# Row marks by 64 small operations that carry the pick's code, in the list part of a hybrid attention and mixture-of-experts kernel

## The chip, the cores and the metric

The kernel runs on one core of one Trainium2 chip. The time is device microseconds of one execution; three runs of the kernel before took 1725.3, 1726.1 and 1726.22 us, so its median is 1726.1 us. The trace is of one further execution, which took 1725.6 us, and whose span from the first to the last instruction is 1723.9 us.

## The reference

The input is x of 4 x 1024 rows with 256 columns, float32. Four layers follow each other, each added to x: a causal attention with 16 heads of 16 (`a`), a mixture of experts (`ffn`), an attention of 8 x 512 rows with one head of 256 (`b`), and the same mixture of experts again. Each is fed a layer norm of x. What matters here is the mixture of experts, which stands twice:

```python
def _moe(t, gate_w, gate_b, mlp1_w, mlp1_b, mlp2_w, mlp2_b):
    logits = t @ gate_w + gate_b                 # 4096 rows, E = 8 experts
    top_v, top_i = jax.lax.top_k(logits, K)      # K = 2 picks for each row
    probs = jax.nn.softmax(top_v, axis=-1)
    w = jnp.zeros((T, E), t.dtype).at[jnp.arange(T)[:, None], top_i].set(probs)
    def body(acc, ew):
        w1, b1, w2, b2, we = ew
        h = _swiglu(t @ w1 + b1)
        y = h @ w2 + b2
        return (acc + we[:, None] * y, None)
```

## The kernel before, in words

The kernel is written engine by engine: each phase is a block in which every engine has its own program, in the order in which the code issues it, and semaphores connect them. No scheduler stands between. At the end of a block all engines meet. The phases are the projections (`a1_`), attention a (`a2_`), its output rows and the logits (`a3_`), the list part (`r1_`), the experts (`e1_`), attention b with its logits (`b_`), the list part again (`r2_`) and the experts again (`e2_`). The trace leaves out the digits: `r_` is the list part in both places, `e_` the experts.

Each of the 4096 rows has two picks, so there are 8192 picks, which lie as 128 partitions by Q = 64 columns. The experts don't compute all rows for all experts: the picks are sorted by expert into MT = 71 tiles of 128 slots, and a tile is computed with one expert's weights. The list part (`rank`, L1132) works out for each pick the slot that it goes to, and then turns this round: for each slot, which pick is in it. The result is the list `token` (128 x 71), which the gathers of the experts need.

Turning it round is a sum of 64 matrix products into one accumulator `p_inv` (128 rows of a tile by 71 tiles). Column q of the picks gives a 128 x 128 matrix of row marks (for each pick a 1 in the column of its row within the tile: `in_row`) and a 128 x 71 matrix of tile marks (a 1 in the column of its tile). Before the change the tile marks are multiplied by the pick's code (`g["marks"]`, a 16 bit integer read as bfloat16), and the product puts the code at its slot (L1340).

The marks are made in five groups of 8, 16, 16, 16 and 8 picks (`BOUNDS`), through two buffers each. The work of a group is shared:

- ScalarE (ACT) spreads the row numbers, each repeated 128 times, into `spread` (L1198).
- VectorE (DVE) compares `slot_tile` with a ramp of tiles into `in_tile` (L1269), multiplies that by the codes into `marked` (L1283), and compares `spread` with the ramp 0 to 127 into `in_row` (L1275). All are `tensor_tensor` operations over 568 to 2048 bfloat16 elements of each partition.
- TensorE (PE) waits for a group's `marked` and `in_row`, and issues its 8 or 16 products.

Behind the marks VectorE adds four tiles of the residual (`X<-X,R`, L1300, `held_added`), and then makes `token` from `p_inv` (L1305), which waits for the last product and for `rows_landed`. GpSimd (POOL) then gathers the first rows (L1367), TensorE turns them (L1459), ScalarE copies them (L1513), and the products of the experts begin (L1470). Beside this ScalarE waits for `held_added` and copies the first expert's weights (L1206).

Of the kernel before, what the change touches and what calls it, by code (L numbers as in the profile page):

```python
# [9 lines left out]
ALU = mybir.AluOpType  # L10
# [1121 lines left out]
def rank(nc, mem, g, t_dram, w_dram, normals):  # L1132
# [3 lines left out]
    QQ = 16  # L1136
    BOUNDS = (0, 8, 24, 40, 56, 64)
# [12 lines left out]
    slot_row = mem.sb("slot_row", [P, Q], BF16)  # L1150
    ramp_tile = mem.sb("ramp_tile", [P, MT, QQ], BF16)
    spread = mem.sb("spread", [P, 2, QQ, P], BF16)
    in_row = mem.sb("in_row", [P, 2, QQ, P], BF16)
    in_tile = mem.sb("in_tile", [P, 2, MT, QQ], BF16)
    marked = mem.sb("marked", [P, 2, MT, QQ], BF16)
# [12 lines left out]
    b_in, ramp_done, slots_done, spread_done, row_done, tile_done, mark_done, inv_done, token_done = (  # L1168
        mem.sem(s) for s in ("b_in", "ramp_d", "slots_d", "spread_d", "row_d", "tile_d", "mark_d", "inv_d", "token_d"))
# [3 lines left out]
    with nc.Block(no_gpsimd_drain=True) as block:  # L1173
# [14 lines left out]
        def _(act):  # L1188
            act.wait_ge(diff_done, 1)
# [3 lines left out]
            act.wait_ge(slots_done, 1)  # L1193
            for k in range(GROUPS):
                n = BOUNDS[k + 1] - BOUNDS[k]
                if k >= 2:
                    act.wait_ge(row_done, k - 1)
                act.copy(spread[:, k % 2, 0:n], slot_row[:, BOUNDS[k]:BOUNDS[k + 1]].unsqueeze(2).to_broadcast([P, n, P])  # L1198
                         ).then_inc(spread_done, 1)
# [9 lines left out]
        def _(dve):  # L1209
# [52 lines left out]
            def at(k):  # L1262
                return slice(BOUNDS[k], BOUNDS[k + 1]), k % 2, BOUNDS[k + 1] - BOUNDS[k]

            def tiles_of(k):
                picks_at, s, n = at(k)
                if k >= 2:
                    dve.wait_ge(mark_done, k - 1)
                dve.tensor_tensor(in_tile[:, s, :, 0:n], slot_tile[:, picks_at].unsqueeze(1).to_broadcast([P, MT, n]),  # L1269
                                  ramp_tile[:, :, 0:n], ALU.is_equal).then_inc(tile_done, 1)  # L1270

            def rows_of(k):
                picks_at, s, n = at(k)
                dve.wait_ge(spread_done, k + 1)
                dve.tensor_tensor(in_row[:, s, 0:n], spread[:, s, 0:n], g["ramp"][:, :].unsqueeze(1).to_broadcast([P, n, P]),  # L1275
                                  ALU.is_equal).then_inc(row_done, 1)

            def marks_of(k):
                picks_at, s, n = at(k)
                if k >= 2:  # L1280
                    dve.wait_ge(inv_done, k - 1)
                dve.wait_ge(tile_done, k + 1)
                dve.tensor_tensor(marked[:, s, :, 0:n], in_tile[:, s, :, 0:n],  # L1283
                                  g["marks"][:, picks_at].unsqueeze(1).to_broadcast([P, MT, n]), ALU.mult
                                  ).then_inc(mark_done, 1)

            tiles_of(0)
            for k in range(GROUPS):
                marks_of(k)
                if k == 0:  # L1290
                    tiles_of(1)
                rows_of(k)
                if k + 2 < GROUPS:
                    tiles_of(k + 2)
# [8 lines left out]
            dve.wait_ge(inv_done, GROUPS)  # L1303
# [12 lines left out]
        def _(pe):  # L1316
# [18 lines left out]
            for k in range(GROUPS):  # L1335
                pe.wait_ge(mark_done, k + 1)
                pe.wait_ge(row_done, k + 1)
                for q in range(BOUNDS[k], BOUNDS[k + 1]):
                    i = q - BOUNDS[k]
                    mm = pe.matmul(p_inv[:, 0:MT], in_row[:, k % 2, i, :], marked[:, k % 2, :, i],  # L1340
                                   start=(q == 0), stop=(q == Q - 1))
# [1077 lines left out]
```

## Time and profile before

| what | value |
|---|---|
| median of three runs | 1726.1 us |
| time of the profiled execution | 1725.6 us |
| its span | 1723.9 us |
| TensorE busy | 1619.6 us (94%), 11174 instructions |
| VectorE busy | 1271.0 us (74%), 2670 instructions |
| ScalarE busy | 1048.6 us (61%) |
| GpSimd busy | 790.2 us (46%) |
| first list part | starts at 647.4 us, its `token` at 669.30 us |
| second list part | starts at 1294.2 us, its `token` at 1316.13 us |

A busy TensorE is not one at its peak, since products are pipelined. Busy shares are means over the whole span; the two list parts are 22 us each of 1724. A row of the timeline gives the start in us, how long the piece is in us, the engine, the line, the operation, its output and inputs, the partitions by elements and their type, and how many instructions are merged in it. The pieces of one engine overlap: the next instruction starts before the one ahead of it has left the pipeline. So there are two readings of an instruction's cost, its duration and the time from its start to the start of the next.

### The profile page before, as it was taken

What the parts mean: (1) busy time and instruction counts of PE and PEld (TensorE: products, weight loads), DVE (VectorE), ACT (ScalarE), POOL (GpSimd) and SP (SyncE); (2) the same over time, 40 slices, a digit from 0 to 9 for tenths busy, and PEclk for the clock granted to TensorE, in tenths of its full rate; (3) what the DMA queues carried; (4) which work ended last, traced back from release to release, by engine and by line L of the source; (5) the groups of instructions that cost most, each with busy time, mean ns of one, the idle gap of its engine ahead of it and who ended that gap; (6) DMA issues with size and microseconds to landing.
All of it is one profiled execution on the core that took longest, in us unless ns stands there. A gap on an engine that the chain in (4) does not pass through costs nothing. (4 is left out here: it accounts for less than half of the span.)

```text
span 1723.9 us, 35933 instructions
## 1 busy us (share of the span) xinstructions
PE 1619.6 (94%) x11174; PEld 1195.5 (69%) x11175; DVE 1271.0 (74%) x2670; ACT 1048.6 (61%) x1850; POOL 790.2 (46%) x768
## 2 busy tenths in 40 slices
PE   8889999999999896999999997799976999999998
PEld 4454444444443685999999997445455999999997
DVE  5688888888884596777777775368897777777775
ACT  4436776776778465666666664557665666666663
POOL 4541111111121132666666664225632766666674
PEclk9999999999999896999999999899976999999999
DMA  5655354453531672332223332301122332222332
GB/s 163 184 148 125 101 129 114 112 125 99 137 105 45 160 248 59 72 49 46 46 48 49 49 47 36 110 1 52 49 74 67 49 49 46 47 47 49 49 48 35
DMA packets 102683, 140.85 MB, mean 82 GB/s; under 512 B 18176, under 2 KB 86784, under 8 KB 99520
## 3 DMA queue, kind: packets, MB, share of 16 engines
q1 hardware_dynamic: 65282, 90.53, 20.0%
q0 software_dynamic: 31808, 37.32, 13.6%
q10 hardware_dynamic: 5502, 11.88, 2.0%
q8 instruction: 45, 0.74, 0.2%
q14 instruction: 46, 0.38, 0.1%
HBM read 74.21 MB, written 56.69 MB: 76 GB/s over the span
## 5 line engine op out<-in xcount | busy, mean ns | idle before, releaser
L633 DVE TENSOR_REDUCE mx<-a_p_sn 128x2 f32<-128x256 f32 (+1 forms) x600 | 333.5, 627 | 60.9 <-PE a_p_sn L670 51.4
L607 ACT ACTIVATE a_Pt<-a_p_st 128x512 f32<-128x512 f32 (+2 forms) x606 | 294.0, 592 | 123.9 <-PE a_p_st L689 123.6
L1521 ACT COPY R<-values_then_w 128x1024 f32 x280 | 279.0, 1044 | 28.2 <-issue 22.2
L1470 PE MATMUL e_p_g<-e_tT,R 128*128 128x128 f32 x2272 | 280.0, 277 | 0.9 <-ACT e_tT L1513 0.9
L1470 PE MATMUL e_p_l<-e_tT,R 128*128 128x128 f32 x2272 | 277.0, 275 | 0.0
L1482 PE MATMUL e_p_y<-w,e_hid 128*128 x1136 | 270.1, 381 | 5.8 <-DVE e_hid L1588 5.8
L1470 PEld LDWEIGHTS e_p_g<-e_tT,R 128*128 128x128 f32 x2272 | 267.8, 194 | 1.8 <-ACT e_tT L1513 1.7
L1470 PEld LDWEIGHTS e_p_l<-e_tT,R 128*128 128x128 f32 x2272 | 265.5, 192 | 0.1
L584 POOL TENSOR_SCALAR_AFFINE_SELECT a_Pt<-a_Pt 128x512 f32<-128x512 f32 x128 | 81.5, 637 | 356.7 <-ACT a_Pt L607 356.7
L1482 PEld LDWEIGHTS e_p_y<-w,e_hid 128*128 128x128 f32 x1136 | 205.6, 191 | 28.4 <-issue 6.2
L670 PE MATMUL a_p_sn<-Kst,Qst 96*128 96x128 bf16 (+1 forms) x720 | 220.0, 332 | 1.8 <-PEq L161 1.8
L689 PE MATMUL a_p_st<-Qst,Kst 99*128 99x512 bf16 (+2 forms) x744 | 205.3, 329 | 6.8 <-DMA Qst<-a_mT 4.1
L1367 POOL DMA_INDIRECT xs<-t_rows,token x142 | 156.6, 1103 | 87.3 <-DVE token L1305 42.0
L1542 ACT ACTIVATE e_sig<-e_glu 128x512 f32<-128x512 f32 x142 | 89.5, 630 | 154.3 <-DVE e_glu L1574 84.5
L1572 DVE TENSOR_TENSOR e_glu<-e_p_g,b 128x512 f32<-128x512 f32 x142 | 98.2, 691 | 106.8 <-PE e_p_g L1470 93.1
L1373 POOL DMA_INDIRECT wt<-pick_weights,pick x142 | 147.7, 1040 | 43.3 <-issue 43.3
L1439 POOL DMA_INDIRECT out<-e_y,result x71 | 115.7, 1629 | 93.0 <-ACT e_y L1529 89.9
L1439 POOL DMA_INDIRECT x_rows<-e_y,result x71 | 115.7, 1630 | 92.0 <-ACT e_y L1529 84.9
L1578 DVE TENSOR_TENSOR e_lin<-e_p_l,b 128x512 f32<-128x512 f32 x142 | 98.2, 692 | 77.0 <-PE e_p_l L1470 75.0
L1529 ACT ACTIVATE e_y<-e_yb,wt 128x256 f32<-128x256 f32 x142 | 72.1, 508 | 129.4 <-DVE e_yb L1555 125.7
L704 PE MATMUL a_p_o<-a_Pt,a_Vst 128*32 128x512 f32 (+3 forms) x1536 | 137.4, 490 | 0.7 <-POOL a_Pt L584 0.7
L670 PEld LDWEIGHTS a_p_sn<-Kst,Qst 96*128 96x128 bf16 x720 | 70.0, 98 | 83.1 <-DVE mx L633 33.8
(266 smaller groups left out, 2381.0 us busy)
## 6 DMA issues: line engine op xcount, KB each, us to landing
qk_parts<-a_part SPq DMA_DIRECT2D x64, 192.0 KB, 3.2
a_Vst<-values_then_w SPq DMA_DIRECT2D x16, 512.0 KB, 18.4
values_then_w<-in_mlp SPq DMA_DIRECT2D x16, 512.0 KB, 4.4
t_rows<-R SPq DMA_DIRECT2D x16, 512.0 KB, 3.2
Kst<-qk_parts SPq DMA_DIRECT2D x14, 384.0 KB
Qst<-qk_parts SPq DMA_DIRECT2D x14, 384.0 KB
o_rows<-a_OT ACTq DMA_DIRECT2D x16, 256.0 KB, 2.0
o_rows<-xs ACTq DMA_DIRECT2D x16, 256.0 KB, 8.0
```

The lines of the kernel that those rows point to most:

```text
L607: act.activation(weights(kb, slice(h, h + n), a, b), key_scores(u, i)[:, 0:n * (b - a)].rearrange("p (n w) -> p n w", n=n), ACT.Exp, scale ...
L633: dve.tensor_reduce(mx[:, hs[0]:hs[-1] + 1, place], p_sn[:, (s + k) % RING, 0:w * len(hs)].rearrange("p (h w) -> p h w", w=w), AX.X, ALU.m ...
L670: mm = pe.matmul(out, Qst[0:ROWS, s, h, qb * P:(qb + 1) * P], Kst[0:ROWS, s, h, k0:k0 + kw], start=True, stop=True, skip_group_check=True)
L689: mm = pe.matmul(key_scores(u, i)[:, j * (b - a):(j + 1) * (b - a)], Kst[0:ROWS + MROWS, s, h0 + j, kb * P:(kb + 1) * P], Qst[0:ROWS + MRO ...
L704: mm = pe.matmul(p_o[PAD * h:PAD * (h + 1), c, a:512], Vst[:, s, kb, PAD * h:PAD * (h + 1)], weights(kb, h, 512 * c + a, 512 * (c + 1)), s ...
L1367: pool.indirect_dma_start(out=g["xs"][:, j % 2, :], out_offset=None, in_=t_dram, in_offset=bass.IndirectOffsetOnAxis(ap=g["token"][:, j:j ...
L1373: pool.indirect_dma_start(out=g["wt"][:, j:j + 1], out_offset=None, in_=w_dram, in_offset=bass.IndirectOffsetOnAxis(ap=g["pick"][:, j:j + ...
L1439: pool.indirect_dma_start(out=acc, out_offset=bass.IndirectOffsetOnAxis(ap=g["result"][:, j:j + 1], axis=0), in_=y[:, j % 2, :], in_offset ...
L1470: mm = pe.matmul(bank[:, s, c * P:(c + 1) * P], copied[:, s, k, at:at + P], tT[:, s, k * P:(k + 1) * P], start=(k == 0), stop=(k == KD - 1))
L1482: mm = pe.matmul(p_y[:, s, 0:D], hid[:, s, k * P:(k + 1) * P], g["w2"][:, bass.ds(e, 1), k, :].rearrange("p a n -> p (a n)"), start=(k == ...
L1521: act.copy(copied[:, s, :, cols], g["w1"][:, bass.ds(e, 1), :, cols].rearrange("p a k n -> p (a k) n")).then_inc(copied_done, 1)
L1572: dve.tensor_tensor(columns(glu), columns(p_g), bias(0), ALU.add).then_inc(g_read, 1)
```

## The change

The row marks now carry the code. One `tensor_scalar` for each of the 64 columns compares the ramp 0 to 127 with the pick's row number and multiplies by its code; both come as operands of one element for each partition (`slot_row[:, q:q + 1]` and `marks[:, q:q + 1]`). These operands are float32, so `slot_row` is written as float32, and ScalarE copies the codes into a float32 `marks` at the start of the block. The five multiplications of tile marks by codes and the five spreads of ScalarE are gone. All marks have buffers of their own (`marked_row` of 64 x 128, `in_tile` of 71 x 64), so VectorE waits for no product. TensorE waits for the tile marks of a group and then for every four row marks. VectorE waits for `slots_done`, the end of `slot_row`, ahead of the first tile marks.

```diff
+    FEW = 4
-    slot_row = mem.sb("slot_row", [P, Q], BF16)
+    slot_row = mem.sb("slot_row", [P, Q])
+    marks = mem.sb("marks", [P, Q])
-    spread = mem.sb("spread", [P, 2, QQ, P], BF16)
-    in_row = mem.sb("in_row", [P, 2, QQ, P], BF16)
-    in_tile = mem.sb("in_tile", [P, 2, MT, QQ], BF16)
-    marked = mem.sb("marked", [P, 2, MT, QQ], BF16)
+    marked_row = mem.sb("marked_row", [P, Q, P], BF16)
+    in_tile = mem.sb("in_tile", [P, MT, Q], BF16)
...
         def _(act):
+            act.copy(marks[:, :], g["marks"]).then_inc(marks_done, 1)
...
-            act.wait_ge(slots_done, 1)
-            for k in range(GROUPS):
-                n = BOUNDS[k + 1] - BOUNDS[k]
-                if k >= 2:
-                    act.wait_ge(row_done, k - 1)
-                act.copy(spread[:, k % 2, 0:n], slot_row[:, BOUNDS[k]:BOUNDS[k + 1]].unsqueeze(2).to_broadcast([P, n, P])
-                         ).then_inc(spread_done, 1)
...
             def tiles_of(k):
-                picks_at, s, n = at(k)
-                if k >= 2:
-                    dve.wait_ge(mark_done, k - 1)
-                dve.tensor_tensor(in_tile[:, s, :, 0:n], slot_tile[:, picks_at].unsqueeze(1).to_broadcast([P, MT, n]),
+                picks_at, n = slice(BOUNDS[k], BOUNDS[k + 1]), BOUNDS[k + 1] - BOUNDS[k]
+                dve.tensor_tensor(in_tile[:, :, picks_at], slot_tile[:, picks_at].unsqueeze(1).to_broadcast([P, MT, n]),
                                   ramp_tile[:, :, 0:n], ALU.is_equal).then_inc(tile_done, 1)
-            def rows_of(k):
...
-            def marks_of(k):
...
+            def marked_rows_of(k):
+                for q in range(BOUNDS[k], BOUNDS[k + 1]):
+                    ins = dve.tensor_scalar(marked_row[:, q, :], g["ramp"][:, :], slot_row[:, q:q + 1], marks[:, q:q + 1],
+                                            ALU.is_equal, ALU.mult)
+                    if q % FEW == FEW - 1:
+                        ins.then_inc(row_done, 1)
+
+            dve.wait_ge(marks_done, 1)
+            dve.wait_ge(slots_done, 1)
             for k in range(GROUPS):
-                marks_of(k)
-                if k == 0:
-                    tiles_of(1)
-                rows_of(k)
-                if k + 2 < GROUPS:
-                    tiles_of(k + 2)
+                tiles_of(k)
+                marked_rows_of(k)
                 if k == 0:
                     dve.wait_ge(expert_done, 1)
...
-            dve.wait_ge(inv_done, GROUPS)
+            dve.wait_ge(inv_done, 1)
...
             for k in range(GROUPS):
-                pe.wait_ge(mark_done, k + 1)
-                pe.wait_ge(row_done, k + 1)
+                pe.wait_ge(tile_done, k + 1)
                 for q in range(BOUNDS[k], BOUNDS[k + 1]):
-                    i = q - BOUNDS[k]
-                    mm = pe.matmul(p_inv[:, 0:MT], in_row[:, k % 2, i, :], marked[:, k % 2, :, i],
+                    if q % FEW == 0:
+                        pe.wait_ge(row_done, q // FEW + 1)
+                    mm = pe.matmul(p_inv[:, 0:MT], marked_row[:, q, :], in_tile[:, :, q],
                                    start=(q == 0), stop=(q == Q - 1))
-                mm.then_inc(inv_done, 1)
+            mm.then_inc(inv_done, 1)
```

The program of VectorE in the first list part of the kernel before, from the first tile marks on (a row is a line of the code, the operation, its output and inputs, and its size):

```order
L1269 TENSOR_TENSOR r_in_tile<-r_slot_tile,r_ramp_tile 128x71x8
L1283 TENSOR_TENSOR r_marked<-r_in_tile,code 128x71x8
L1269 TENSOR_TENSOR r_in_tile<-r_slot_tile,r_ramp_tile 128x1136
L1275 TENSOR_TENSOR r_in_row<-r_spread,ramp 128x1024
L1269 TENSOR_TENSOR r_in_tile<-r_slot_tile,r_ramp_tile 128x1136
L1297 TENSOR_SCALAR expert<-r_p_e 1x71
L1283 TENSOR_TENSOR r_marked<-r_in_tile,code 128x1136
L1275 TENSOR_TENSOR r_in_row<-r_spread,ramp 128x2048
```

The same place in the changed kernel, up to the list (x8 and x16 are so many of them in a row):

```order
L1258 TENSOR_TENSOR r_in_tile<-r_slot_tile,r_ramp_tile 128x71x8
L1263 TENSOR_SCALAR r_marked_row<-ramp,r_slot_row,r_marks 128x128 x8
L1275 TENSOR_SCALAR expert<-r_p_e 1x71
L1258 TENSOR_TENSOR r_in_tile<-r_slot_tile,r_ramp_tile 128x71x16
L1263 TENSOR_SCALAR r_marked_row<-ramp,r_slot_row,r_marks 128x128 x16
```

Before, 15 operations make all marks of a list; now five make the tile marks, and 64 stand behind them in pieces of 8, 16, 16, 16 and 8. The residual's addition is still the last operation ahead of `token`.

The program of TensorE in the first list part of the changed kernel, from the first product on (in brackets the semaphores that it waits for); before, the first row of each group stood there with waits for both kinds of marks, and 7 or 15 products without a wait behind it:

```order
L1318 MATMUL r_p_inv<-r_in_tile,r_marked_row 128x71 [waits r1_row_d,r1_tile_d]
L1318 MATMUL r_p_inv<-r_in_tile,r_marked_row 128x71 x3
L1318 MATMUL r_p_inv<-r_in_tile,r_marked_row 128x71 [waits r1_row_d]
L1318 MATMUL r_p_inv<-r_in_tile,r_marked_row 128x71 x3
L1318 MATMUL r_p_inv<-r_in_tile,r_marked_row 128x71 [waits r1_row_d,r1_tile_d]
```

The 64 products are the same in number and size; what moved is that they may start by fours.

## Rows read from the trace of the kernel before

**Rows 1.** The page: span, and busy time by engine.
```profile
span 1723.9 us, 35933 instructions
PE 1619.6 (94%) x11174; PEld 1195.5 (69%) x11175; DVE 1271.0 (74%) x2670; ACT 1048.6 (61%) x1850; POOL 790.2 (46%) x768
```

**Rows 2.** Chain of waits in the second list part: start, us, what.
```profile
1303.05 0.23 DVE r_slot_row L1258
1303.27 0.37 DVE r_in_tile L1269
...
1310.57 5.47 PE r_p_inv L1340 x40
1316.13 0.24 DVE token L1305
...
1316.64 2.94 DMA xs<-t_rows,token
```

**Rows 3.** Timeline of the first list part, from the slots to the list.
```profile
656.22 0.23 DVE L1258 SCALAR_TENSOR_TENSOR r_slot_row<-r_slot_tile,r_slot 128x64 bf16<-128x64 bf16 x1
656.36 0.45 DVE L1269 TENSOR_TENSOR r_in_tile<-r_slot_tile,r_ramp_tile 128x568 bf16<-128x568 bf16 x1
...
658.70 1.20 PE L1340 MATMUL r_p_inv<-r_marked,r_in_row 128*128 128x71 bf16 x8 [4.39 <-DVE r_in_row L1275]
659.13 0.21 DVE L1297 TENSOR_SCALAR expert<-r_p_e 1x71 int32<-1x71 f32 x1
659.28 0.73 DVE L1283 TENSOR_TENSOR r_marked<-r_in_tile,code 128x1136 bf16<-128x1136 bf16 x1
...
661.07 0.73 DVE L1269 TENSOR_TENSOR r_in_tile<-r_slot_tile,r_ramp_tile 128x1136 bf16<-128x1136 bf16 x1
...
661.73 0.73 DVE L1283 TENSOR_TENSOR r_marked<-r_in_tile,code 128x1136 bf16<-128x1136 bf16 x1
...
667.00 1.22 DVE L1300 TENSOR_TENSOR X<-X,R 128x1024 f32<-128x1024 f32 x1
669.28 1.99 ACT L1206 COPY R<-values_then_w 128x1024 f32 x2 [4.61 <-issue]
669.30 0.23 DVE L1305 TENSOR_SCALAR token<-r_p_inv 128x71 int32<-128x71 int32 x1 [1.08 <-PE r_p_inv L1340]
669.45 0.22 DVE L1307 TENSOR_SCALAR pick<-r_p_inv 128x71 int32<-128x71 int32 x1
```

**Rows 4.** Timeline of VectorE: two stretches with one-element operands.
```profile
6.55 0.73 DVE L314 TENSOR_SCALAR a_n<-X,a_mv,a_rstd 128x256 f32<-128x256 f32 x2
...
653.38 0.23 DVE L1248 TENSOR_SCALAR r_passed<-r_cnt,spare 128x8 bf16<-128x8 f32 x1
653.52 0.42 DVE L1250 TENSOR_TENSOR r_cum<-r_p_c,r_cnt 128x256 f32<-128x256 f32 x1
```

**Rows 5.** Groups of VectorE by shape: count, busy us, mean ns of one, idle before.
```profile
L314 DVE TENSOR_SCALAR a_n<-X,a_mv,a_rstd 128x256 f32<-128x256 f32 x4 | 1.5, 408 | 0.1
...
L1574 DVE TENSOR_SCALAR e_glu<-e_glu 128x512 f32<-128x512 f32 x142 | 61.2, 431 | 4.8
...
L1256 DVE TENSOR_SCALAR r_whole_tile<-r_slot 128x64 f32<-128x64 f32 x2 | 0.4, 194 | 0.1
...
L1275 DVE TENSOR_TENSOR r_in_row<-r_spread,ramp 128x2048 bf16<-128x2048 bf16 x6 | 7.2, 1206 | 0.0
...
L1275 DVE TENSOR_TENSOR r_in_row<-r_spread,ramp 128x1024 bf16<-128x1024 bf16 x4 | 2.7, 682 | 0.0
```

**Rows 6.** Timeline of the first list part's front: ScalarE.
```profile
647.35 1.28 ACT L1190 ACT_TABLE_LOAD   x1 [3.56 <-PEq L820]
...
651.19 0.23 ACT L1190 ACTIVATE r_diff<-r_diff 128x32 f32<-128x32 f32 x1 [2.56 <-DVE r_diff L1230]
```

**Rows 7.** Behind the first list: ScalarE's copy, then the experts' first products.
```profile
673.58 0.37 ACT L1513 COPY e_tT<-e_p_t 128x256 f32<-128x256 f32 x1 [2.31 <-PE e_p_t L1459]
...
674.00 3.79 PE L1470 MATMUL e_p_g<-e_tT,R 128*128 128x128 f32 x16 [0.46 <-ACT e_tT L1513]
```

More of the change, by code:

```diff
@@ L1167, in rank @@
         mem.sem(s) for s in ("diff_d", "exp_d", "picks_d", "far_d", "cnt_d", "passed_d", "expert_d"))
-    b_in, ramp_done, slots_done, spread_done, row_done, tile_done, mark_done, inv_done, token_done = (
-        mem.sem(s) for s in ("b_in", "ramp_d", "slots_d", "spread_d", "row_d", "tile_d", "mark_d", "inv_d", "token_d"))
+    b_in, ramp_done, marks_done, slots_done, row_done, tile_done, inv_done, token_done = (
+        mem.sem(s) for s in ("b_in", "ramp_d", "marks_d", "slots_d", "row_d", "tile_d", "inv_d", "token_d"))
     w_done, wt_done, wT_done, w_out = (mem.sem(s) for s in ("w_d", "wt_d", "wT_d", "w_out"))
@@ L1260, in _ @@
             dve.wait_ge(ramp_done, 1)
-            def at(k):
-                return slice(BOUNDS[k], BOUNDS[k + 1]), k % 2, BOUNDS[k + 1] - BOUNDS[k]
             def tiles_of(k):
-                picks_at, s, n = at(k)
-                if k >= 2:
-                    dve.wait_ge(mark_done, k - 1)
-                dve.tensor_tensor(in_tile[:, s, :, 0:n], slot_tile[:, picks_at].unsqueeze(1).to_broadcast([P, MT, n]),
+                picks_at, n = slice(BOUNDS[k], BOUNDS[k + 1]), BOUNDS[k + 1] - BOUNDS[k]
+                dve.tensor_tensor(in_tile[:, :, picks_at], slot_tile[:, picks_at].unsqueeze(1).to_broadcast([P, MT, n]),
                                   ramp_tile[:, :, 0:n], ALU.is_equal).then_inc(tile_done, 1)
-            def rows_of(k):
[L1273 to L1276, printed above, removed]
-            def marks_of(k):
[L1279 to L1287, printed above, removed]
-            for k in range(GROUPS):
-                marks_of(k)
-                if k == 0:
-                    tiles_of(1)
-                rows_of(k)
-                if k + 2 < GROUPS:
-                    tiles_of(k + 2)
+            def marked_rows_of(k):
[6 more added lines that the diff above has]
+            dve.wait_ge(slots_done, 1)
+            for k in range(GROUPS):
+                tiles_of(k)
+                marked_rows_of(k)
                 if k == 0:
```

## The prediction

> **What bounds the kernel now.** I read the page first: TensorE is busy 94% of the span and VectorE 74% [rows 1]. These shares come from the long phases. The change lies in the two list parts, of 22 us each, so the next view is the chain of waits there. It runs through VectorE from `r_slot_row` to the marks, then through the last 40 products of `p_inv` (5.47 us), `token`, the gather (2.94 us) and the first products of the experts [rows 2]. No other work of the kernel goes on beside it: what the list takes longer, the kernel takes longer, twice. The reader is to see in the timeline [rows 3] that from the start of `slot_row` (656.22) to the start of `token` (669.30) are 13.08 us. VectorE is through with its marks at 667.00, where the residual's addition starts; that ends at 668.22, 1.08 us before `token`, so it lies hidden under TensorE's tail. In the second list part the same two starts are 1303.05 and 1316.13, again 13.08 [rows 2], so one sum serves for both.
>
> **What changes order.** TensorE no longer sets the end if the marks come slower than it eats them. It takes 5.47/40 = 0.137 us a product in its unbroken tail [rows 2]. Now each product needs one operation of VectorE of its own. So the question is what one `tensor_scalar` of 128 bfloat16 elements with two one-element operands costs, from start to start.
>
> **The price s of one row mark.** The kernel before has one operation of that kind: the layer norm's, 256 float32 elements with two such operands. Two of them in a row take 0.73 us [rows 4] and one lasts 408 ns [rows 5], so the second starts 0.73 - 0.408 = 0.322 us behind the first. How much of that goes by elements? Without such operands the same kind takes 431 ns for 512 and 194 ns for 64 elements [rows 5], so 237/448 = 0.53 ns each, 0.135 us for 256. The rest, 0.187 us, is fixed. That it is the operands which make it large is borne out by a second row: `r_passed`, one such operand and 8 elements, lasts 0.23 us, and the next starts 0.14 behind it [rows 4]; less 0.004 for its elements that is 0.136. Against it stands `token`, with none: 0.15 from start to start for 71 elements [rows 3]. At 1.02 ns an element, twice the slope of 1206 - 682 = 524 ns for 1024 bfloat16 elements of a two-input operation [rows 5], 71 take 0.073, which leaves 0.077. So the fixed part is 0.077 with none, 0.136 with one and 0.187 with two, some 0.055 for each.
>
> The 128 elements of a row mark are bfloat16. No row shows this kind in bfloat16. Two-input operations take 0.51 ns for a bfloat16 element, and the residual's addition in float32 1219 ns for 1024 [rows 3], about double. If the kind here halves too, 128 elements take 128 x 0.53/2 = 0.034 us. I take s = 0.187 + 0.034 = 0.221 us. The bounds are 0.077 + 0.034 = 0.111 (operands free when queued) and 0.187 + 128 x 1.02 ns = 0.318 (one element at a time). I choose near the two-operand row, since it is the same operation with the same operands. The Trainium skill, VectorE: DVE Perf Modes, section on the perf-mode tier table, gives `tensor_scalar` on bfloat16 in SBUF 4 elements a cycle and float32 2, which is the halving assumed; no row here shows the 4.
>
> **The sum for one list**, from the start of `slot_row` to the start of `token`:
> - `slots_done`: VectorE now waits for the end of `slot_row`, 0.23 and some 0.03 to go on, 0.26. Before, the tile marks started 0.14 behind [rows 3].
> - Tile marks: two groups of 8 at 0.37 [rows 2], three of 16 at 0.66 (661.07 to 661.73, [rows 3]): 2.72.
> - `expert` between them: 0.15 (659.13 to 659.28, [rows 3]).
> - 64 row marks at 0.221: 14.14.
> - The residual's addition, now bare: 1.22 less the 0.08 by which the next instruction starts before its end, 1.14 [rows 3].
>
> Together 4.27 + 64 s = 18.41 us, against 13.08: 5.33 longer. Two lists: 10.7 us.
>
> **Why the rest costs or gives nothing.** Gone are five multiplications by codes (0.45 to 0.73 us each) and five comparisons of spread rows on VectorE; they are in the 13.08, and the sum replaces them. ScalarE's five spreads go too, but they lay beside VectorE, which in [rows 3] never stands idle for them. TensorE: four products take 0.55 us and four marks 0.88, so it waits for VectorE at each four. Behind the last mark it needs about 0.15 to begin, 3 x 0.137 more, and 0.31 for the last one, 0.87 in all, under the 1.14 of the residual's addition. That cover is thin: without it `token` would come 0.8 later than the last mark. Starting by fours lets TensorE begin early, but an early start helps only the engine that ends last, and that is no longer TensorE. The codes' copy on ScalarE (64 elements, about as long as the 0.23 exponential) stands ahead of a table load of 1.28 us; both are through by about 649, and the exponential waits until 651.19 [rows 6]. `held_added` comes together with `token`; ScalarE's weight copies then run from the same moment as `token` (669.28 and 669.30 before too, [rows 3]) and end 2 us later, ahead of the copy of the gathered rows at 673.58 [rows 7]. So everything behind `token` shifts by as much as it does.
>
> The profiled execution took 1725.6 us, the median of the runs is 1726.1. From the first the sum gives 1736.3, on the median 1736.8. I forecast 1736.8 us.
>
> **Rivals.**
> - *Operands free when queued (faster).* If the fetch of the two operands is hidden behind the operation ahead, s = 0.111. Then VectorE's path is 4.27 + 7.10 = 11.37, and TensorE, starting at about 1.2 us (0.26 + 0.37 + 4 x 0.111 + 0.15) and taking 64 x 0.137 = 8.77, ends at 10.0 + 0.3, before it. Each list gains 1.7: 1722.7 us. It wins from s below (13.08 - 4.27)/64 = 0.138. For it: `token`, which has no such operand, is queued at this price [rows 3]. Against it: the layer norm's pair stood in a queue just so, and took 0.322. The Trainium skill, Vector Engine (DVE) Microarchitecture Reference, section 5.2 Measured stream behaviour on trn2, gives built-in one- and two-source ops about 75 ns an instruction after queue overlap, which would lead here; the trace agrees for `token` (0.077) and not for the layer norm's pair (0.187). Chance 0.08.
> - *One operand's price only.* With 0.136 fixed, s = 0.170, path 15.15, 2.07 more a list: 1730.2 us. Against it the two-operand row. Chance 0.12.
> - *No halving for bfloat16.* s = 0.187 + 0.068 = 0.255, path 20.6, 7.5 a list: 1741.1 us. For it: no row shows the faster mode. Chance 0.14.
> - *One element at a time.* s = 0.318, path 24.6, 11.5 a list: 1749.2 us. Against it 431 ns for 512 elements. Chance 0.04.
> - *TensorE binds.* It now reads tile marks 64 elements apart instead of 16. It decides from 0.22 us a product; at the 0.31 that one lasts alone, 64 take 19.8, some 9 more a list: 1744 us. No row bears on it. Chance 0.04.
>
> My forecast has 0.58, and by itself ranges from 1733 to 1740: s from 0.195 to 0.245, since the row is of 256 float32 elements, and up to 0.5 us for each start of the experts, whose first 16 products take 3.79 us here [rows 7]. The range to hold 8 in 10 takes in the case without halving and nearly the one-operand case: 1729.5 to 1742. What can be told from no change is about 0.2%, 3.5 us, thus s between 0.111 and 0.165. The free-operand case lies on that border: 0.05 of its 0.08 is faster, with 0.01 for the unforeseen; same gets its rest and a half of the one-operand case, 0.09; slower 0.85.
>
> **What would show it.** In the changed profile: 64 `r_marked_row` in each list, starts 0.22 us apart and about 0.31 us long (0.034 + 0.08 + 0.187); TensorE waiting for VectorE before every four products; the residual's addition ending where `token` starts; 18.4 us between `slot_row` and `token` in both lists; the same distance from `token` to the experts as before. Starts under 0.138 apart would make the forecast wrong in sign, over 0.25 in size; unchanged marks but a late `token` behind idle VectorE would name TensorE.

## The result

The changed kernel takes 1739.6 us, the median of four runs (1737.1 to 1740.0), against 1725.7 (1724.4 to 1726.2) for the kernel before beside it. The ratio is 1.0076, with a 95% interval of 1.0064 to 1.0088: 13.1 us more, between 11.0 and 15.2. The forecast was 1736.8, in a range from 1729.5 to 1742, with 0.85 for slower. The profiled execution took 1739.75 us, its span 1738.0 is 14.1 over that of before. Taken once more beside other runs of the kernel before (after_again, below), the changed kernel was 16.0 us over, between 12.8 and 19.3.

The page of the changed kernel answers to [rows 1]: span, and busy time by engine.
```profile
span 1738.0 us, 36028 instructions
PE 1624.0 (93%) x11174; PEld 1192.2 (69%) x11175; DVE 1285.3 (74%) x2778; ACT 1030.8 (59%) x1842; POOL 797.2 (46%) x768
```
VectorE is busy 14.3 us more and the span is 14.1 longer, which looks like one and the same thing. It isn't quite, as the account of the two spans, further down, shows.

### The profile page after: what moved, and what is told of

Same layout as the page of the kernel before. It is cut to its first block and busy times, and to the rows that moved or that the text cites. A ratio compares the mean times of both kernels' runs of the same rounds, so it can differ in the third digit from the quotient of the medians.

```text
span 1738.0 us, 36028 instructions
## 1 busy us (share of the span) xinstructions
PE 1624.0 (93%) x11174; PEld 1192.2 (69%) x11175; DVE 1285.3 (74%) x2778; ACT 1030.8 (59%) x1842; POOL 797.2 (46%) x768
## 5 line engine op out<-in xcount | busy, mean ns | idle before, releaser
L1345 POOL DMA_INDIRECT xs<-t_rows,token x142 | 161.8, 1139 | 98.8 <-DVE token L1283 53.1
L1417 POOL DMA_INDIRECT x_rows<-e_y,result x71 | 119.3, 1680 | 84.7 <-ACT e_y L1507 72.4
```

The costliest lines, as they stand in the source:

```text
L1345: pool.indirect_dma_start(out=g["xs"][:, j % 2, :], out_offset=None, in_=t_dram, in_offset=bass.IndirectOffsetOnAxis(ap=g["token"][:, j:j ...
L1417: pool.indirect_dma_start(out=acc, out_offset=bass.IndirectOffsetOnAxis(ap=g["result"][:, j:j + 1], axis=0), in_=y[:, j % 2, :], in_offset ...
```

## The profile after: the list

The timeline of the first list part, which answers to [rows 3] (start, us, engine, line, operation, output and inputs, shapes, count, and in brackets the idle time before and its releaser).
```profile
655.39 0.23 DVE L1252 SCALAR_TENSOR_TENSOR r_slot_row<-r_slot_tile,r_slot 128x64 f32<-128x64 bf16 x1
655.76 0.46 DVE L1258 TENSOR_TENSOR r_in_tile<-r_slot_tile,r_ramp_tile 128x568 bf16<-128x568 bf16 x1
656.13 1.87 DVE L1263 TENSOR_SCALAR r_marked_row<-ramp,r_slot_row,r_marks 128x128 bf16<-128x128 bf16 x8
...
657.91 0.21 DVE L1275 TENSOR_SCALAR expert<-r_p_e 1x71 int32<-1x71 f32 x1
658.06 0.73 DVE L1258 TENSOR_TENSOR r_in_tile<-r_slot_tile,r_ramp_tile 128x1136 bf16<-128x1136 bf16 x1
...
672.89 1.21 DVE L1278 TENSOR_TENSOR X<-X,R 128x1024 f32<-128x1024 f32 x1
...
673.03 0.65 PE L1318 MATMUL r_p_inv<-r_in_tile,r_marked_row 128*128 128x71 bf16 x4 [0.16 <-DVE r_marked_row L1263]
674.03 0.21 DVE L1283 TENSOR_SCALAR token<-r_p_inv 128x71 int32<-128x71 int32 x1
```
And what TensorE waits for in that stretch: us in total, times, longest.
```profile
PE r_p_inv L1318 <- DVE r_marked_row L1263: 9.8, 16, 3.8
```
TensorE waits for VectorE 16 times, once for each four marks, and VectorE never waits once it has begun. From `slot_row` (655.39) to `token` (674.03) are 18.64 us, and 18.64 again in the second list (1309.63 to 1328.27), against 13.08 before. Eight marks and the step to `expert` take 657.91 - 656.13 = 1.78, so a mark follows the one ahead by 0.223 us. The sum with measured terms: 0.37 until the first tile marks, 2.72 for tile marks, 0.15 for `expert`, 64 x 0.223 = 14.27, 1.14 for the residual's addition, together 18.65. The last four products end at 673.68, inside the addition, as forecast.

## The profile after: behind the list

The same view, from `token` on. It answers to the last part of [rows 3] and to [rows 7].
```profile
675.16 1.99 ACT L1200 COPY R<-values_then_w 128x1024 f32 x2 [22.74 <-issue]
...
678.09 0.94 POOL L1351 DMA_INDIRECT wt<-pick_weights,pick  x1 [1.14 <-POOLq L1173]
...
678.77 3.44 PE L1448 MATMUL e_p_g<-e_tT,R 128*128 128x128 f32 x16 [0.46 <-ACT e_tT L1491]
...
682.27 1.95 PE L1448 MATMUL e_p_l<-e_tT,R 128*128 128x128 f32 x16
...
686.94 1.04 ACT L1499 COPY R<-values_then_w 128x1024 f32 x1 [1.22 <-remote]
686.96 0.69 DVE L1556 TENSOR_TENSOR e_lin<-e_p_l,b 128x512 f32<-128x512 f32 x1 [3.41 <-remote]
687.13 0.95 POOL L1345 DMA_INDIRECT xs<-t_rows,token  x1 [1.85 <-remote]
...
689.13 0.69 DVE L1566 TENSOR_TENSOR e_hid<-e_lin,e_sig 128x512 f32<-128x512 f32 x1
```
The same operations in the kernel before:
```profile
672.55 0.94 POOL L1373 DMA_INDIRECT wt<-pick_weights,pick  x1 [0.30 <-issue]
...
677.58 0.63 PE L1459 MATMUL e_p_t<-ident,xs 128*128 128x128 f32 x2
678.01 2.07 PE L1470 MATMUL e_p_l<-e_tT,R 128*128 128x128 f32 x16
...
680.71 0.69 DVE L1578 TENSOR_TENSOR e_lin<-e_p_l,b 128x512 f32<-128x512 f32 x1 [1.61 <-PE e_p_l L1470]
...
682.62 0.69 DVE L1588 TENSOR_TENSOR e_hid<-e_lin,e_sig 128x512 f32<-128x512 f32 x1
```
Two distances differ that were forecast to be the same. ScalarE's weight copies start 1.13 us behind `token`, before 0.02 ahead of it. The first `e_hid` starts 15.10 behind `token` (689.13 - 674.03), before 13.32. In the second list it is 14.49 against 12.01. Between the two stands GpSimd's first gather of weights, behind the end of the block at which all engines meet: 4.06 behind `token` (678.09), before 3.25 (672.55).

In the second list of the kernel before the view names what the weight copies waited for, the residual's addition:
```profile
1315.86 1.99 ACT L1206 COPY R<-values_then_w 128x1024 f32 x2 [4.36 <-DVE X L1300]
```
In the first list the products themselves are not what is late: those of `e_p_l` start 8.24 behind `token` (before 8.71) and end by the record at 684.22, but `e_lin`, which reads them, starts 2.74 after that; before it was 0.63 after. In the second list they end 0.69 later against `token` (10.64, before 9.95), and `e_lin` starts 1.94 after their end instead of 0.15. The granted clock of TensorE has a part in this. It goes from its lower level (0.50, 1.2 GHz) to its upper (1.00, 2.4 GHz) 7.7 and 8.8 us behind `token` in the changed kernel, 8.9 and 7.2 in the one before, each time after TensorE had worked at the experts' first products since 4.6 to 4.7. In the profiled executions of all kernels here this moment lies anywhere from 7.0 to 10.4. The rise gave something back in the first list and can account for the 0.69 of the second (an estimate: 1.6 us longer at half the clock are 0.8 us of work), but not for the late `e_lin`.

The account of the two spans, in us, as differences after minus before:

| stretch | first | second | sum |
|---|---|---|---|
| front, up to the list part (after 646.61, before 647.43) | | | -0.8 |
| `slot_row` to `token` | 5.55 | 5.56 | 11.1 |
| `token` to the first `e_hid` | 1.79 | 2.48 | 4.3 |
| first to last of 71 `e_hid` (before 385.75, 386.23) | -0.15 | -0.63 | -0.8 |
| part between the expert phases | | | 0.2 |
| all | | | 14.0 |

So the marks are 11.1 of it. A second loss of 4.3 sits behind `token`, and some 0.8 of that is given back while the experts run.

## Experiments: the price of a mark

The list was forecast from s, the time from one mark's start to the next. Three kernels change the mark alone.

**no_operand.** The changed kernel with constants in the place of both operands.
```diff
-   ins = dve.tensor_scalar(marked_row[:, q, :], g["ramp"][:, :], slot_row[:, q:q + 1], marks[:, q:q + 1],
+   ins = dve.tensor_scalar(marked_row[:, q, :], g["ramp"][:, :], 5.0, 1.0,
```


> The changed kernel with two constants (5 and 1) in place of the row number and the code in the 64 row marks; it leaves out the right list, so the gathers read other rows, while the number of instructions is the same. Theory of the operands (0.055 us for each one-element operand, also in a queue): the marks start 0.11 us apart instead of 0.223, and slot_row to token is 4.27 + 64 x 0.11 = 11.3 us, 7.3 less than in the changed kernel, 1.8 less than before; the time is some 14 to 15 us under the changed kernel's, 1722 to 1726. Rival (the price is that of a short operation in this kind and does not go by operands): starts stay 0.22 apart and the time stays at 1739.5.

**float_ramp.** The changed kernel with a float32 ramp as input of the marks.
```diff
+    rampf = mem.sb("rampf", [P, P])
-   ins = dve.tensor_scalar(marked_row[:, q, :], g["ramp"][:, :], slot_row[:, q:q + 1], marks[:, q:q + 1],
+   ins = dve.tensor_scalar(marked_row[:, q, :], rampf[:, :], slot_row[:, q:q + 1], marks[:, q:q + 1],
```


> The changed kernel with the ramp that the row marks read in float32 instead of bfloat16 (made by a second iota on GpSimd at the start of the block); all else the same. If the elements go at 0.26 ns each in bfloat16 and 0.53 in float32, starts are 0.223 + 0.034 = 0.257 us apart, slot_row to token 18.64 + 2.2 = 20.8 us, the time 4.4 us more, 1744. If the kind does not go faster in bfloat16 at all (so that 0.223 is 0.155 fixed and 0.068 for elements), it stays at 0.223 and 1739.5.

**one_operand_coded.** The codes back on the tile marks, multiplied in place, so that a row mark has one operand.
```diff
+   dve.tensor_tensor(in_tile[:, :, picks_at], in_tile[:, :, picks_at],
+                     g["marks"][:, picks_at].unsqueeze(1).to_broadcast([P, MT, n]), ALU.mult).then_inc(tile_done, 1)
-   ins = dve.tensor_scalar(marked_row[:, q, :], g["ramp"][:, :], slot_row[:, q:q + 1], marks[:, q:q + 1],
-                           ALU.is_equal, ALU.mult)
+   ins = dve.tensor_scalar(marked_row[:, q, :], g["ramp"][:, :], slot_row[:, q:q + 1], None, ALU.is_equal)
```


> The changed kernel with the codes put back on the tile marks (a second operation in place on each group), so that the 64 row marks have one one-element operand and one comparison. Measured so far: 0.102 us from start to start with none, 0.223 with two. If each operand costs the same, 0.163; with one or both at one price, 0.22; if one costs nothing, 0.10. The list at 0.163: 0.37 for the wait, 0.48 + 0.37 twice and 0.76 + 0.66 three times for tile marks and codes, 0.15, 10.4, 1.14, in all 18.0 us against 18.64.

The groups of VectorE by shape (count, busy us, mean ns of one, idle before): the changed kernel,
```profile
L1263 DVE TENSOR_SCALAR r_marked_row<-ramp,r_slot_row,r_marks 128x128 bf16<-128x128 bf16 x128 | 29.3, 298 | 0.0
```
the one without operands,
```profile
L1263 DVE TENSOR_SCALAR r_marked_row<-ramp 128x128 bf16<-128x128 bf16 x128 | 13.8, 177 | 0.0
```
the one with one operand,
```profile
L1267 DVE TENSOR_SCALAR r_marked_row<-ramp,r_slot_row 128x128 bf16<-128x128 bf16 x128 | 21.7, 248 | 0.0
```
and the one with the float32 ramp.
```profile
L1264 DVE TENSOR_SCALAR r_marked_row<-r_rampf,r_slot_row,r_marks 128x128 bf16<-128x128 f32 x128 | 33.5, 330 | 0.0
```
From start to start, read off unbroken runs of marks:

| kernel | operands | input | start to start | `slot_row` to `token` | median of runs |
|---|---|---|---|---|---|
| no_operand | 0 | bf16 | 0.102 | 10.90 | 1721.2 (ratio 0.9988, 0.9976 to 1.0000) |
| one_operand_coded | 1 | bf16 | 0.163 | 18.07 | 1733.3 (one run) |
| after | 2 | bf16 | 0.223 | 18.64 | 1739.6 |
| float_ramp | 2 | f32 | 0.256 | 20.76 | 1740.6 (one run) |

No_operand came out a little under what was expected of it (0.102 for 0.11, a list of 10.90 for 11.3, 1721.2 for 1722 to 1726); one_operand_coded came out as expected but for 0.07 in the list. An operand of one element for each partition costs 0.061 and 0.060 us, in a full queue too. One_operand_coded also drops the multiplication from the mark, so its step alone could be part operand and part multiplication; no_operand, which keeps both operations, shows that two operands together are 0.121. The float32 input adds 0.033 for 128 elements, the halving that the forecast assumed (0.034). What is left with no operand is 0.102 - 0.034 = 0.068. In the list without operands the change would gain 2.2 us a list; with one operand the marks are 3.8 cheaper (64 x 0.06), but five multiplications, each of which waits for its own tile marks, take back 3.3 of that. The total of float_ramp, 1740.6 for an expected 1744, is low for its list: its front part was 643.1 us, 3.5 shorter than that of after. The front varies from 642.4 to 648.8 between the profiled executions of these kernels, all of which have nearly the same work there. So lists are compared here by their own stretch, and totals only by medians with an interval.

**by_groups.** The changed kernel, with TensorE waiting once for each group of 8 or 16 marks instead of for every four.
```diff
-   if q % FEW == FEW - 1:
-       ins.then_inc(row_done, 1)
+   ins.then_inc(row_done, 1)      # behind the loop
...
+   pe.wait_ge(row_done, k + 1)    # behind the wait for the tile marks
-   if q % FEW == 0:
-       pe.wait_ge(row_done, q // FEW + 1)
```


> The changed kernel with one part undone: TensorE waits for all row marks of a group instead of every four. By my reckoning only the last group matters: behind the last mark stand 8 products instead of 4, 0.15 + 7 x 0.137 + 0.31 = 1.42 us against the 1.14 of the residual's addition, so slot_row to token is 18.8 to 18.9 us instead of 18.64. A rival that holds the early start for worth something in the middle of the list expects 20 or more.

Its timeline at the end of the first list:
```profile
671.72 1.21 DVE L1277 TENSOR_TENSOR X<-X,R 128x1024 f32<-128x1024 f32 x1
...
671.94 1.13 PE L1316 MATMUL r_p_inv<-r_in_tile,r_marked_row 128*128 128x71 bf16 x8
673.19 0.23 DVE L1282 TENSOR_SCALAR token<-r_p_inv 128x71 int32<-128x71 int32 x1 [0.26 <-PE r_p_inv L1316]
```
The list takes 18.96, 0.3 more, and 0.1 over what was expected: only the last group's tail sticks out, here 8 products. Starting by fours is worth 0.3 us a list and no more, since TensorE is not what ends last. One run gave 1737.3 us.

**in_order.** The kernel before with the three steps of each group in one order, to see whether the freer order of the changed kernel had something of its own to give.
```diff
-            tiles_of(0)
             for k in range(GROUPS):
+                tiles_of(k)
                 marks_of(k)
-                if k == 0:
-                    tiles_of(1)
                 rows_of(k)
-                if k + 2 < GROUPS:
-                    tiles_of(k + 2)
```


> The kernel before with tile marks, codes and row marks of each group made in this order, so that the second group's tile marks no longer stand ahead of the first group's row marks. Row marks of groups 1 and 2 come some 0.5 us earlier, bounded by ScalarE's spreads; TensorE is unbroken from the third group on and ends the list, so slot_row to token is 12.5 us instead of 13.1 and the time about 1 us less than before. If ScalarE's spreads bind instead, 13.1 or a little more, and no change.

```profile
651.17 0.23 DVE L1258 SCALAR_TENSOR_TENSOR r_slot_row<-r_slot_tile,r_slot 128x64 bf16<-128x64 bf16 x1
...
653.35 1.20 PE L1336 MATMUL r_p_inv<-r_marked,r_in_row 128*128 128x71 bf16 x8 [4.08 <-DVE r_in_row L1275]
...
656.05 2.25 PE L1336 MATMUL r_p_inv<-r_marked,r_in_row 128*128 128x71 bf16 x16 [1.50 <-DVE r_in_row L1275]
...
657.35 1.22 DVE L1275 TENSOR_TENSOR r_in_row<-r_spread,ramp 128x2048 bf16<-128x2048 bf16 x1
658.48 0.74 DVE L1269 TENSOR_TENSOR r_in_tile<-r_slot_tile,r_ramp_tile 128x1136 bf16<-128x1136 bf16 x1
...
659.33 0.75 DVE L1283 TENSOR_TENSOR r_marked<-r_in_tile,code 128x1136 bf16<-128x1136 bf16 x1
```
This expectation was wrong: the list takes 13.59, 0.5 longer. TensorE begins 2.18 behind `slot_row` instead of 2.48, but each multiplication by codes now follows the very tile marks that it reads and comes up to 0.85 behind them (658.48 to 659.33), where 0.66 is enough when another operation stands between. That this is what makes the list longer is read off the timeline and was not tested. The time is unchanged: 1724.4, ratio 0.9999 (0.9989 to 1.0010).

## Experiments: what is late behind the list

In the kernel before the residual's addition, and with it `held_added`, ended 1.08 ahead of `token`; in the changed kernel it ends with `token`. ScalarE waits for it before it loads the expert's number and copies weights. The theory: the late copies cost what is lost behind `token`. Its rival, called theory C in the expectations, was that a burst is at fault: the late copies, GpSimd's gathers and SyncE's write of 512 KB of `X` now fall together. (The write itself didn't move: SyncE issues it behind its eight loads, 8.90 us behind `token` in both kernels in the first list.)

**x_first.** The changed kernel with the residual's addition ahead of the marks.
```diff
+            dve.tensor_tensor(g["X"][:, HELD:NT, :], g["X"][:, HELD:NT, :], g["R"][:, normals, :], ALU.add
+                              ).then_inc(held_added, 1)
             dve.wait_ge(marks_done, 1)
...
-            dve.tensor_tensor(g["X"][:, HELD:NT, :], g["X"][:, HELD:NT, :], g["R"][:, normals, :], ALU.add
-                              ).then_inc(held_added, 1)
             dve.wait_ge(rows_landed, 1)
```


> The changed kernel with the residual's addition moved ahead of the marks (behind the slots), so that held_added comes some 17 us before token. Nothing else is moved; VectorE has the same work before token. From slot_row to token I expect 18.6 us less the 0.1 by which TensorE's last four products are shorter than the addition, 18.5. Theory A (the loss of 1.9 us behind each list comes from held_added coming with token: ScalarE's two weight copies end 1.1 us later against token, the block's end and GpSimd's next gathers 0.8 us later): the way from token to the end of the first e_hid returns from 15.8 us to about 14.0, the whole is 3.5 to 4 us faster than the changed kernel, near 1736. Theory B (the loss comes from something else: the clock's rise, code fetched at another moment, the changed place of tiles): it stays at 15.8 and the time at about 1739.5.

```profile
653.85 1.22 DVE L1268 TENSOR_TENSOR X<-X,R 128x1024 f32<-128x1024 f32 x1
654.99 0.45 DVE L1258 TENSOR_TENSOR r_in_tile<-r_slot_tile,r_ramp_tile 128x568 bf16<-128x568 bf16 x1
...
672.24 0.65 PE L1318 MATMUL r_p_inv<-r_in_tile,r_marked_row 128*128 128x71 bf16 x4 [0.16 <-DVE r_marked_row L1263]
673.00 0.23 DVE L1283 TENSOR_SCALAR token<-r_p_inv 128x71 int32<-128x71 int32 x1 [0.82 <-PE r_p_inv L1318]
...
683.42 0.69 DVE L1556 TENSOR_TENSOR e_lin<-e_p_l,b 128x512 f32<-128x512 f32 x1 [0.84 <-issue]
...
685.34 0.69 DVE L1566 TENSOR_TENSOR e_hid<-e_lin,e_sig 128x512 f32<-128x512 f32 x1
```
Behind the list it did as the theory says: `e_hid` 12.33 and 13.05 behind `token`, about where the kernel before has it. In the list the expectation was wrong: 19.30, 0.66 more than after. The addition's 1.14 is on the path at either place; moved ahead it hides the 0.23 of waiting for `slot_row`, and TensorE's tail behind the last mark, 0.88, comes bare: 0.88 - 0.23 = 0.65. The median was 1736.3, ratio 1.0065 (1.0048 to 1.0082), some 2 to 3 us under after although its lists are 1.3 longer; its interval overlaps that of after, so this gain rests on the distances in the trace more than on the times.

**act_late** and **act_late_again.** The kernel before, in which ScalarE waits for `token` too. The second run was taken to see whether the late `e_lin` belongs to the kernel or to one execution.
```diff
             act.wait_ge(held_added, 1)
+            act.wait_ge(token_done, 1)
```


> The kernel before, with one wait more: ScalarE's first weight copies wait for token_done too, so they start about 1.1 us behind the start of token instead of beside it. The marks and the list are as before, 13.08 us. Theory A: the start of the experts loses about 1.8 us in each of the two lists without any change of the marks, 1729.3 us against 1725.7, and GpSimd's first gather of weights starts 4.1 us behind token instead of 3.25. Theory B: it stays within 0.5 us of before in each, at most 1726.7.

> The kernel of act_late once more, to tell whether the late e_lin belongs to a kernel with late weight copies or to an execution. In 13 profiles so far either both lists show e_lin at 12.5 to 12.9 us after token or neither does; those with it all have late copies (start 0.9 us or more behind token), but three kernels with such late copies don't show it. If it belongs to the kernel, both lists show 12.6 to 12.9 again and the median is 2 to 3 us over before. If it is chance in each execution, it may show 10.1 to 11.6, and the times spread over two levels some 4 us apart.

```profile
669.55 0.23 DVE L1306 TENSOR_SCALAR token<-r_p_inv 128x71 int32<-128x71 int32 x1 [1.09 <-PE r_p_inv L1341]
...
670.87 1.99 ACT L1207 COPY R<-values_then_w 128x1024 f32 x2 [5.95 <-issue]
...
682.47 0.69 DVE L1579 TENSOR_TENSOR e_lin<-e_p_l,b 128x512 f32<-128x512 f32 x1 [3.42 <-remote]
...
684.65 0.69 DVE L1589 TENSOR_TENSOR e_hid<-e_lin,e_sig 128x512 f32<-128x512 f32 x1
```
Lists of 13.09, as before, and behind them the changed kernel's picture to a tenth: `e_lin` 12.92 and 12.63 behind `token` (after: 12.93 and 12.58), `e_hid` 15.10 and 14.55 (after: 15.11 and 14.49), released "remote" as there (a releaser that the view can't name). The repeat has 15.15 and 14.54. The medians are 1728.1 and 1727.4, against 1725.2 both times, the ratio 1.0014 both times (1.0002 to 1.0026 and 1.0003 to 1.0024): 2.4 us for one wait, with no change in the list. **after_again**, the changed kernel once more, has 14.95 and 14.39.

> The changed kernel once more, beside both_late on one chip. From its lists it is 11.1 us over before. If the loss at the experts' start (1.8 us in a list) happens in some executions and not in others, the profile of this one may show e_lin at 10.5 to 11.6 or at 12.5 to 12.9 us after token, the list 18.64 in either case, and the median lies 11 to 14.5 us over before.

Its median was 1742.1, ratio 1.0093 (1.0074 to 1.0112), which is 16.0 us over before and more than the 11 to 14.5 that were expected; its lists took 18.63 and 18.64. What makes up the excess was not found. The loss behind `token` is there in every one of the four profiles of these two kernels, in both lists.

**store_late**, **before_store_late** and **both_late.** The same line in the changed kernel, in the kernel before, and in act_late: SyncE's write of `X` waits for the first `e_hid`.
```diff
+            sp.wait_ge(hid_done, 1)
             sp.dma_start(acc[HELD * P:T, :].rearrange("(t p) d -> p t d", p=P), g["X"][:, HELD:NT, :]).then_inc(held_out, 16)
```


> The changed kernel, in which SyncE's 512 KB write of the four added tiles, issued 8.9 us after token before, waits for the first e_hid. Theory C (in both kernels the first products of the experts are signalled late while SyncE's eight loads of b2 and this write fill the DMA engines, until 12.6 us after token; the gather that comes 0.8 us later only makes it hit): the burst ends some 3 us earlier, the first e_lin from products starts 10.5 to 11.2 us after token instead of 12.9 and 12.6, and the time is 3 to 4 us under the changed kernel's, about 1736. Theory D (it is the late gather of the third tile itself that costs): e_lin stays at 12.5 to 12.9 and the time at 1739.

> The same edit to the kernel before. There e_lin starts 11.4 and 10.1 us after token. Theory C: at most 0.5 us to gain in each list, 1724.5 to 1725.5, and nothing lost elsewhere. Theory D: 1725.2, unchanged.

> The kernel before with ScalarE's weight copies late as in act_late and SyncE's write late as in store_late. Theory C (late copies cost only through the gather that falls into SyncE's burst): e_lin at 10.2 to 11.3 us after token though the copies start 1.1 us behind it, 1724 to 1725.5, against 1728.1 for act_late. Theory D (late copies cost by themselves): 12.5 to 12.9, and about 1728.

The first list of store_late:
```profile
670.34 0.21 DVE L1283 TENSOR_SCALAR token<-r_p_inv 128x71 int32<-128x71 int32 x1
...
680.52 0.69 DVE L1557 TENSOR_TENSOR e_lin<-e_p_l,b 128x512 f32<-128x512 f32 x1 [0.85 <-PE e_p_l L1449]
```
and that of both_late:
```profile
668.47 0.23 DVE L1306 TENSOR_SCALAR token<-r_p_inv 128x71 int32<-128x71 int32 x1 [1.09 <-PE r_p_inv L1341]
...
681.39 0.69 DVE L1580 TENSOR_TENSOR e_lin<-e_p_l,b 128x512 f32<-128x512 f32 x1 [3.02 <-remote]
```
Store_late alone would have made theory C look proven: with the write away, `e_lin` comes 10.18 and 10.71 behind `token`, and the median is 1734.7, ratio 1.0059 (1.0042 to 1.0075). But both_late has the write away just the same, and its `e_lin` comes at 12.92 and 12.64. A burst that needs the write can't be the cause. Theory C fell, by where `e_lin` stands and not by the time: both_late's median lies between what the two theories expected, and its interval holds both the kernel before and act_late. Before_store_late shows no change (1724.3, ratio 1.0002, 0.9991 to 1.0013); both_late 1726.5, ratio 1.0006 (0.9995 to 1.0016).

Nor are late copies enough by themselves. All kernels side by side, us behind `token`, first list / second list:

| kernel | copies start | `e_lin` | `e_hid` |
|---|---|---|---|
| before | -0.02 / -0.27 | 11.41 / 10.10 | 13.32 / 12.01 |
| in_order | 0.18 / -0.08 | 11.62 / 9.91 | 13.56 / 11.83 |
| before_store_late | -0.03 / -0.27 | 10.22 / 10.83 | 12.13 / 12.76 |
| x_first | -14.74 / -14.98 | 10.42 / 11.14 | 12.33 / 13.05 |
| by_groups | 0.80 / 0.56 | 10.62 / 11.29 | 12.54 / 13.23 |
| store_late | 1.13 / 0.89 | 10.18 / 10.71 | 12.09 / 12.62 |
| no_operand | 1.13 / 0.89 | 11.56 / 11.34 | 13.48 / 13.26 |
| one_operand_coded | 1.14 / 0.90 | 11.63 / 11.00 | 13.54 / 12.91 |
| after | 1.13 / 0.89 | 12.93 / 12.58 | 15.11 / 14.49 |
| float_ramp | 1.13 / 0.89 | 12.75 / 12.50 | 14.93 / 14.41 |
| act_late | 1.31 / 1.07 | 12.92 / 12.63 | 15.10 / 14.55 |
| both_late | 1.31 / 1.07 | 12.92 / 12.64 | 15.09 / 14.56 |

Every kernel with an `e_lin` over 12 has late copies, and none with early ones has it. Yet by_groups, store_late, no_operand and one_operand_coded have late copies and no late `e_lin`.

One more reading of the traces divides the kernels. Beside the instructions a trace keeps moments at which semaphores change (the counters by which engines and DMAs tell each other that they are done). Counted from 7 to 12 us behind each `token`, the repeats in brackets:

| kernels | changes recorded in a list | `e_lin` behind the recorded end of its products, us |
|---|---|---|
| after, act_late, both_late, float_ramp | 18 to 27 (20 to 24) | 1.23 to 2.74 (2.02 to 2.83) |
| before, in_order, x_first, no_operand | 38 to 52 | 0.15 to 0.63 |
| by_groups, store_late, before_store_late, one_operand_coded | 170 to 213 | 0.14 to 0.51 |

In the last group the products' own semaphore changes 0.01 to 0.02 us after their recorded end. In the other two there are stretches, most of them of 0.6 to 0.8 us, without any recorded change, and then a few together. In the changed kernel's first list the semaphore of `e_p_l` changes 12.80 behind `token`, 2.61 after the products' recorded end, and `e_lin` starts 0.13 later: what it waits for is that late change. The kernels of the middle group have late readers too, one step further on: in the second list of the kernel before the next `e_glu` starts 2.46 after its products ended (1330.55 and 1328.09). Store_late differs from after by more than the moved write, since it is in the last group, while both_late, with the same line added, is in the first. The record has holes there as well: the change that released the first `e_glu` of the changed kernel, in time at 8.34 behind `token`, isn't in it, so the counts are no measure of how many changes there were. What puts a kernel into a group was not tested, nor whether the sparse changes make the readers late or only come with them. That link stays open.

## Why the prediction was right, and where it was not

- **The bound moves to VectorE: right.** TensorE waits before every four products, VectorE runs without a gap.
- **s = 0.221: right.** It is 0.223, and a mark is 298 ns long. The forecast said about 0.31, but its own terms (0.034 + 0.08 + 0.187) add up to 0.301. The reading of the layer norm's pair [rows 4] as a fixed part of 0.187 with some 0.055 for each operand held for another shape and type: 0.223 - 0.034 = 0.189, and 0.06 each. The rivals with s = 0.111, 0.170, 0.255 and 0.318 are out. The first of them is near what no_operand measures, 0.102: it is the price without operands.
- **The skill's 75 ns, weighed in the prediction.** No_operand shows a fixed part of 0.068; with two operands it is 0.189. The Trainium skill, Vector Engine (DVE) Microarchitecture Reference, section 5.2 Measured stream behaviour on trn2, has about 75 ns an instruction; the trace agrees with it for marks with constants and not for marks with operands.
- **The halving for bfloat16, which no row of before showed: right.** Float_ramp against after is 0.033 us for 128 elements.
- **The sum for one list, 18.41: 0.23 short.** Of that 0.13 is s (64 x 0.002), and 0.11 the wait for the end of `slot_row`, 0.37 from start to start instead of 0.26. Two lists: 11.1 us instead of 10.7.
- **TensorE's tail, 0.87, under the addition's 1.14: right.** In x_first, where it is bare, it is 0.88. (The rival in which TensorE binds was priced at some 9 us a list; its own terms, a start at 1.66 and 19.8 of products, come to 8.4. It didn't happen.)
- **"So everything behind `token` shifts by as much as it does": wrong.** This is the step that failed. The prediction took the copies' start, 669.28 beside `token` at 669.30 [rows 3], as an effect of `token`. In truth both follow the addition: it ends at 668.22, and the copy starts 1.06 later; in the changed kernel it ends at 674.10 and the copy starts at 675.16, 1.06 later again. In the second list of before the trace names the addition as the copies' releaser. The addition had been hidden 1.08 ahead of `token`, and ScalarE used exactly that lead. With the lead gone the copies start 1.13 behind `token` and the first `e_hid` comes 1.8 and 2.5 later. Act_late puts that delay alone into the kernel before and shows the whole shift; x_first gives the lead back and takes it away. Shown is that in these two pairs the shift comes and goes with the lead. The lost lead alone does not decide it: by_groups, store_late, no_operand and one_operand_coded have lost it too, and their first `e_hid` comes at most 0.2 later in the first list and 0.6 to 1.3 in the second. Not shown is the mechanism from late copies to a late `e_lin`.
- **The total.** 10.7 was forecast and 13.1 (11.0 to 15.2) measured. The marks' 11.1 lies at the lower end of that interval. With 4.3 for the start of the experts less 0.8 given back it is 14.6, inside it, and inside that of after_again (12.8 to 19.3), which the marks alone are under. The range, up to 1742, had room for this loss only because it took in the case without halving, which isn't what happened. Store_late, without the late start and with the marks kept, measured 10.2 (7.2 to 12.9). The forecast's range allowed "up to 0.5 us for each start of the experts"; they were 3.6 and 5 times that.

No version beat the kernel before: before_store_late and in_order are level with it, and the one under it, no_operand, leaves out what makes the list.

## What to carry to other kernels

Before one wide operation is cut into many narrow ones, multiply their number by the start-to-start time of a pair of the same kind with the same operands, here 0.10 us with constants, 0.16 with one operand of one element for each partition and 0.22 with two: 64 of them cost more than the five wide multiplications and comparisons that they replaced. When the engine that ends last changes, look at each operation that was hidden in the old wait, and at whoever waits for that one: a small lead that nobody wrote down (1.08 us here) can be what starts the next phase in time. Two things that start within two hundredths of a microsecond of each other are not cause and effect until the releaser of each has been found.

## What the runs showed of the hardware

- Operands of one element for each partition are not hidden by the queue: in runs of 8 and 16 marks, 0.102, 0.163 and 0.223 us from start to start, so 0.06 us for each operand of each mark.
- A completed product can be seen by its readers 2.7 us after its recorded end, with ScalarE, VectorE and GpSimd all released "remote" within 0.2 us of each other (686.94, 686.96 and 687.13 in the changed kernel). It was stable over repeats of two kernels and absent in others with the same delay of the copies. It goes with stretches of 0.6 to 0.8 us in which the trace records no change of any semaphore: 18 changes from 7 to 12 us behind `token` in the changed kernel's first list, 193 in store_late's. Its cause is open.
- The part ahead of the first list varied from 642.4 to 648.8 us between profiled executions, though the kernels differ there by no more than a copy of 64 elements or a ramp of 128. A single total therefore could not tell 3 us here; the stretch from `slot_row` to `token` repeated within 0.02.
